# Local attention with two key tiles: the mask added by VectorE together with the maximum

## The reference, cut to what matters

```python
qb = q.reshape(B, H, nb, bs, dk)                 # bs = window = 128
kw = jnp.concatenate([kp[:, :, :-1], kp[:, :, 1:]], axis=3)   # the tile before, the own tile
scores = jnp.einsum('bhnrd,bhncd->bhnrc', qb, kw) * scale
dist = bs + r - c
key_global = i * bs - bs + c
valid = (dist >= 0) & (dist <= window) & (key_global >= 0)
scores = jnp.where(valid[None, None], scores, jnp.finfo(scores.dtype).min)
probs = jax.nn.softmax(scores, axis=-1)
out = jnp.einsum('bhnrc,bhncd->bhnrd', probs, vw)
```

## Time and profile before

| | |
|---|---|
| three runs | 428.84, 430.21, 435.47 us (median 430.21) |
| the profiled execution | 430.3 us, its span 428.5 us |
| mean granted TensorE clock | 0.941 of full speed |
| busy, share of the span | PE 84%, PEld 53%, DVE 72%, ACT 48%, POOL 26% |
| stage 4's 24 items | about 132.8 to 226 us of the span |

### The profile page before, as it was taken

How to read it: one execution, slowest core, us unless ns; L and a number is a source line. 1 busy time by engine, 2 the same in 40 slices (tenths; PEclk the granted TensorE clock), 3 DMA queues, 4 the chain that set the end, 5 groups by cost and what they waited for, 6 DMA issues and landing times.

```text
span 428.5 us, 6958 instructions
## 1 busy us (share of the span) xinstructions
PE 361.4 (84%) x2412; PEld 226.6 (53%) x2438; DVE 307.1 (72%) x652; ACT 207.2 (48%) x549; POOL 110.3 (26%) x214
## 2 busy tenths in 40 slices
PE   8897958699977999989977566678989889999992
PEld 3544646544434576656654332436756645677682
DVE  4998788999725487897888987797988365323245
ACT  2773401260035665775544757889999443110100
POOL 8437777656571000000020111121111000000003
PEclk9999985979999599999998979899999999999998
DMA  7994111731670000020015698999979700511221
GB/s 208 388 366 85 3 1 1 223 72 24 151 315 0 2 2 2 0 50 2 2 27 75 121 162 164 153 165 150 158 142 161 226 3 14 147 49 50 73 74 49
DMA packets 90306, 43.52 MB, mean 102 GB/s; under 512 B 78944, under 2 KB 86048, under 8 KB 89824
## 3 DMA queue, kind: packets, MB, share of 16 engines
q1 hardware_dynamic: 87968, 43.02, 42.8%
q0 software_dynamic: 2304, 0.07, 1.5%
HBM read 21.58 MB, written 2.88 MB: 57 GB/s over the span
## 4 chain that ended last, share of the span: by engine, by line
PE 50%; DVE 14%; DMA 11%; issue 9%; ACT 9%; POOL 5%; SPq 1%; POOLq 0%; DVEq 0%; ACTq 0%
PE ps L833 25%; DMA area_b<-area_a 6%; PE ps L1308 6%; ACT area_a L743 5%; PE ps L1067 5%; PE ps L1078 4%; POOL deltas L536 3%; PE ps L997 2%; PE ps L1061 2%; DMA early<-in_w_qkv_dram 2%; DMA area_b<-deltas 2%; DVE area_a L1700 2%; ACT area_a L718 2%; DMA deltas<-entry_w,small 1%; DVE stats L1431 1%
## 5 line engine op out<-in xcount | busy, mean ns | idle before, releaser
L1700 DVE CUSTOM_DVE_ANT_0 area_a<-ps,zero,small 128x1024 f32<-128x1024 f32 x64 | 79.6, 1275 | 11.2 <-PE ps L1128 8.3
L743 ACT ACTIVATE area_a<-area_a,small 128x1024 int16<-128x1024 f32 x64 | 73.2, 1144 | 21.9 <-POOL small L592 12.8
L718 ACT ACTIVATE area_a<-ps,small 128x256 f32<-128x256 f32 (+1 forms) x128 | 52.0, 430 | 31.9 <-DVE small L1642 28.2
L833 PE MATMUL ps<-xT_odd,early 128*128 128x128 f32 (+2 forms) x248 | 61.8, 393 | 4.7 <-ACT area_a L754 1.9
L514 POOL TENSOR_SCALAR var_eps<-meanvar 128x1 f32<-128x1 f32 x24 | 7.5, 313 | 187.4 <-DVE meanvar L1432 187.3
L833 PEld LDWEIGHTS ps<-xT_odd,early 128*128 128x128 f32 x248 | 38.7, 191 | 26.0 <-ACT area_a L754 5.5
L1642 DVE TENSOR_REDUCE small<-ps 128x4 f32<-128x1024 f32 (+1 forms) x24 | 29.3, 1221 | 20.2 <-PE ps L1067 20.1
L592 POOL TENSOR_SCALAR small<-small 128x1 f32<-128x1 f32 x64 | 12.7, 198 | 87.8 <-DVE small L1700 87.6
L833 PE MATMUL ps<-area_b,xT_even 128*128 128x512 f32 x64 | 30.0, 633 | 5.0 <-ACT area_b L695 5.0
L1783 DVE TENSOR_TENSOR area_b<-ps,area_b 128x384 f32<-128x384 f32 (+1 forms) x16 | 9.2, 573 | 33.7 <-ACT area_b L801 33.7
L1651 DVE COPY area_b<-ps 128x512 f32<-128x512 f32 x48 | 30.9, 680 | 1.6 <-PE ps L1078 1.4
(11 more groups left out here) (285 smaller groups left out, 633.4 us busy)
## 6 DMA issues: line engine op xcount, KB each, us to landing
early<-in_w_up_dram SPq DMA_DIRECT2D x1, 4096.0 KB, 12.6
area_b<-gates_out SPq DMA_DIRECT2D x16, 256.0 KB, 3.0
deltas<-area_b SPq DMA_DIRECT2D x1, 2112.0 KB, 14.6
area_b<-deltas SPq DMA_DIRECT2D x2, 1024.0 KB, 6.3
area_a<-in_w_down_dram SPq DMA_DIRECT2D x1, 2048.0 KB, 9.5
area_b<-area_a SPq DMA_TRANSPOSE x67, 3.3
early<-in_ctxT_dram SPq DMA_DIRECT2D x1, 1024.0 KB, 11.2
early<-in_ctx_dram SPq DMA_DIRECT2D x1, 1024.0 KB
```

Of the source, the lines that this page charges most:

```text
L718: a = act.activation(p1[:, n % 2, x * nk * P:(x + 1) * nk * P], scores1(n)[:, x * nk * P:(x + 1) * nk * P], ACT.Exp, bias=nmx1[:, n % 2, x ...
L743: act.activation(px[:, u % PX, :], sx[:, u % 3, :], ACT.Exp, bias=nbx[:, u:u + 1], accum_out=zx[:, i, h:h + 1]).then_inc(sem("px_ready"), 1)
L833: mm = pe.matmul(dst, lhsT(c), rhs(c), start=start and c == 0, stop=stop and c == DC - 1, **kw)
L1700: dve.tensor_tensor_reduce(sx[:, u % 3, :], bank(2 * (u % 2), 2), zero[:].broadcast_to([P, B * M]), qsc[:, i, h:h + 1], LOWEST, ALU.add, A ...
```

## The change

For items of an odd tile, TensorE no longer writes the mask; the products of queries and keys begin their banks (`start=True`). VectorE, in place of the one maximum, runs one `tensor_tensor_reduce` a head over 256 columns: it adds `window` to the scores, negates the sum, writes it to SBUF into the item's place for weights, and takes the minimum, which is the negated maximum. ScalarE then takes the exponentials in place, SBUF to SBUF, with `scale=-1`. Scores(n+2) wait for `max1_ready` of item n instead of `p1_ready` if item n is of an odd tile. The place for weights is now one of three (`weights1`), the third in `area_b`; who first writes it waits for the turn of item n-3 (`p1_free`). Items of an even tile keep mask, maximum, exponentials and wait as they were, with the three places.

```diff
-        p1 = carve("a", 18 * N, [2, 8 * P])
+        p1 = [carve("a", 18 * N, [8 * P]), carve("a", 20 * N, [8 * P]), carve("b", 10 * N, [8 * P])]
...
+        def masked_by_vector(n):
+
+            return items1[n][0] % 2 == 1
+
+        def weights1(n):
+            return p1[n % 3]
+
+        def p1_free(eng, n):
+
+            if n >= 3:
+                eng.wait_ge(sem("pT1_ps"), 2 * (n - 2))
+
+        def scores1_free(eng, n):
+
+            if masked_by_vector(n):
+                eng.wait_ge(sem("max1_ready"), n + 1)
+            else:
+                eng.wait_ge(sem("p1_ready"), 2 * (n + 1))
...
                     act.wait_ge(sem("max1_ready"), n + 1)
-                    if n >= 2:
-
-                        act.wait_ge(sem("pT1_ps"), 2 * (n - 1))
+                    p1_free(act, n)
+                    by_vector = masked_by_vector(n)
+                    src = weights1(n) if by_vector else scores1(n)
...
-                        a = act.activation(p1[:, n % 2, x * nk * P:(x + 1) * nk * P], scores1(n)[:, x * nk * P:(x + 1) * nk * P],
-                                           ACT.Exp, bias=nmx1[:, n % 2, x:x + 1], accum_out=z1[:, i, h:h + 1])
+                        own = slice(x * nk * P, (x + 1) * nk * P)
+                        a = act.activation(weights1(n)[:, own], src[:, own], ACT.Exp, scale=-1.0 if by_vector else 1.0,
+                                           bias=nmx1[:, n % 2, x:x + 1], accum_out=z1[:, i, h:h + 1])
...
                     if n >= 2:
-
-                        pe.wait_ge(sem("p1_ready"), 2 * (n - 1))
+                        scores1_free(pe, n - 2)
                     heads = slice(hh * HU // nk, (hh + 1) * HU // nk)
-                    for x in range(2):
-                        pe.matmul(bank(2 * (n % 2) + x), ident_b[:], window[:, nk - 1, :], start=True, stop=False)
+                    by_vector = masked_by_vector(n)
+                    if not by_vector:
+                        for x in range(2):
+                            pe.matmul(bank(2 * (n % 2) + x), ident_b[:], window[:, 0, :], start=True, stop=False)
...
-                                           start=False, stop=b == nk - 1)
+                                           start=by_vector, stop=True)
...
+                    if masked_by_vector(n):
+                        p1_free(dve, n)
+                        for x in range(8 // nk):
+                            own = slice(x * nk * P, (x + 1) * nk * P)
+                            m = dve.tensor_tensor_reduce(weights1(n)[:, own], scores1(n)[:, own], window[:, 1, 0:nk * P], -1.0, -LOWEST,
+                                                         ALU.add, ALU.min, nmx1[:, n % 2, x:x + 1])
+                        m.then_inc(sem("max1_ready"), 1)
+                        return
```

More of the change, by code:

```diff
@@ L1077, in turn @@
                         for y in range(4):
-                            mm = pe.transpose(bank(4 + x)[:, y * P:(y + 1) * P], p1[:, n % 2, (4 * x + y) * P:(4 * x + y + 1) * P], ident[:])
+                            mm = pe.transpose(bank(4 + x)[:, y * P:(y + 1) * P], weights1(n)[:, (4 * x + y) * P:(4 * x + y + 1) * P], ident[:])
                         mm.then_inc(sem("pT1_ps"), 1)
```

## The result

| kernel | median us | lowest to highest | ratio to before, 95% interval |
|---|---|---|---|
| before (beside the first series) | 430.36 | 428.84 to 435.47 | |
| changed, first series | 426.71 | 424.15 to 430.56 | 0.9898 [0.9851, 0.9944] |
| changed, repeat (e1_again) | 427.51 | 423.38 to 435.73 | 0.9926 [0.9888, 0.9965] |
| changed, third series (e11_changed) | 427.09 | 422.42 to 429.86 | 0.9896 [0.9820, 0.9971] |

The change makes the kernel faster by 0.7 to 1.0%, 3 to 4.5 us. 425.2 us was forecast, 1.2% less than before. The ratios leave out executions in the chip's slower state, the first profiled one of the changed kernel (430.56 us) among them, while the medians hold all. Lengths of stretches are read from the repeats' profiles where nothing else is said.

The account below looks back on a forecast made before the run. TensorE was taken to bound the odd-tile stretches, the engines coming out level after the change. Gains of 2.9 and 2.5 us, less 0.3, took 430.3 to 425.2 us; own range 423.7 to 426.6, 8-in-10 range 423.0 to 432.0.

Parts of the forecast that it names:

- TensorE full, VectorE with 6 us to spare: Odd-tile stretches of local attention: TensorE busy 26.36 of 27.0 and 26.57 of 27.1 us, VectorE with 6 us left in each.
- 0.43 us of masks an item: Two mask products of 512 columns taken off TensorE per odd item: 3.4 us a stretch, 6.9 us in all.
- 0.35 us a head, from the 512-column row: VectorE's step per 256-column fused operation, ends 0.33 and 0.40; four take 1.41 us for 1.14, +0.27 an item.
- No penalty for exponentials out of SBUF: ScalarE reading the fused result from SBUF: no penalty to be seen, and even 0.1 us more on each hidden.
- The pair at 5.3 us: Two successive odd-tile items in the chain of waits: 5.3 us against 6.15 before.
- The walk: Stepping VectorE and TensorE through a pair of items at the new prices: free at 3.2 us, done at 3.4.
- the lump "for what neither can hide": First odd stretch: 1.2 us added to the fuller engine's 22.9, for waits in four pairs and VectorE's normalising work.
- The piece between only shifts: Even-tile items between the odd stretches keep masks and waits; item 16's scores still wait 2.92 us, this piece only shifts.
- The sum, 5.1 us: Total stage gain: 2.9 us in the first odd stretch, 2.5 in the second, less 0.3 for the last maximum.
- The whole gain is let through: Stage 5, behind the changed stage, is a chain of queues without a fixed date; the whole gain reaches the end.
- rival (a): VectorE's heads cost 0.40 us, +0.46 an item: gain 3.1 us, time 427.1 us; chance 0.19.
- The clock rival (e): TensorE's granted clock falls in a stretch because it waits more; 10 us of work at half speed: 435 us; chance 0.04.

Follow-up runs that it names:

- e11_changed: The changed kernel itself a third time, no edit, timed beside the kernel with both fillings: 427.09 us, ratio 0.9896.
- e2: Kernel before with TensorE's mask products left out for odd tiles and nothing in their place, so those rows are unmasked: ratio 0.9852, 6.4 us.
- e3: Changed kernel with TensorE's mask products put back for the odd tiles, so the mask is added twice: ratio 1.0004.
- e4: Changed kernel with one fused operation of 1024 columns for each odd item in place of four of 256: ratio 0.9916, 426.81 us.
- e11: Short spelling for the third series of the changed kernel, no edit: 427.09 us, ratio 0.9896.
- e10: Changed kernel with the first filling alone, 11 unread TensorE products of 512 columns behind the scores of item 1: ratio 0.9895.
- e7: Kernel before with both fillings, unread TensorE products: 11 of 512 columns behind item 1's scores, 8 of 256 ahead of item 16's: ratio 1.0031.

## Why the prediction was right, point by point

- **TensorE full, VectorE with 6 us to spare**: right for the first stretch, shown by e2 (TensorE's work off: 6.4 us) and e3 (VectorE's on, TensorE's kept: nothing). In the second the 6 us were an average: for 8 us VectorE was full as well (under e2), which the table doesn't show.
- **0.43 us of masks an item**: right on average, 6.42 us for 15 items in e2. It is 0.47 where TensorE alone is late: behind an apply the masks held 0.38 us and the 0.16 of issue ahead of it, 0.54, and 0.43 at the other item. Behind item 16 it is 0.37.
- **0.35 us a head, from the 512-column row**: right to the hundredth. Step 0.345, because the accumulator read does overlap with the next head, as in all rows of before; an item's maximum costs 1.38 us for 1.14. The last hundredths were luck: the 0.35 was taken with one column per nanosecond, which no row shows (the rows' slope is 0.58 us for 512 columns, 1.13 ns each, and gave 0.33). The row of the other fused operation at the right width (0.40) was the wrong one to trust; the same operation at the wrong width was nearer. The Trainium skill's formula for VectorE out of PSUM ("VectorE: DVE Perf Modes", The TRN2 errata) gives an estimate of 0.39 us for 256 columns, between this step and the 0.42 of a single operation's duration; the measured step decides, and it is cheaper. Worked out again, the forecast by that formula would be 1.8 us later, not 1.5.
- **No penalty for exponentials out of SBUF**: there is one. A duration grows by 24 to 28 ns (501 and 497 for 473), and the step from one head's start to the next by 0.04 us, from 0.45 to 0.49 (152.27 and 152.72 before, 167.29 and 167.78 in e1_again). That is 0.16 us an item, hidden as the bound of 0.1 each had allowed: in e1_again the odd items' scores are held up by the exponentials at one place only, the gap ahead of item 16, as before. The Trainium skill ("VectorE: DVE Perf Modes", The TRN2 errata) states a larger fixed part for ScalarE out of SBUF than out of PSUM, 224 against 172 cycles, an estimate of 43 ns at its 1.2 GHz; the step agrees with it, the duration shows a bit over half.
- **The pair at 5.3 us**: 5.18 where TensorE is late; where VectorE is, 159.10 - 153.41 = 5.69 between the maxima of items 5 and 7 in e1_again, of which 0.26 + 0.28 are the tile's own work (the reciprocal and a copy). The walk ended with VectorE waiting 0.2 us on TensorE and left that work to the lump "for what neither can hide".
- **That lump, 1.2 us in the first stretch, is the term that was mis-sized.** Against the masks' 3.4 us a stretch it left a loss of 0.5 us in the first and 0.9 in the second. The runs show 1.07 and 0.68 (the table under e2). In the first stretch it was too small by about 0.6 us; e4, with 0.18 us less on VectorE for each item, got 0.95 of the 1.07 back.
- **The piece between only shifts**: it became 0.84 us shorter. 0.55 of it is item 16's masks, which stood in the chain behind ScalarE's release (0.60 us to the first score product) and which the prediction had counted in the second stretch; the rest, 0.29, is the maximum of item 12, for which VectorE is late in the changed kernel.
- **The sum, 5.1 us**: forecast were 5.4 for 16 items, less 0.3 for the last maximum; measured are 4.68 for 15 of them, less 0.24. Item 4's masks lie in the piece from item 0, whose length varies too much from profile to profile to show them.
- **The whole gain is let through**: right. From item 23's maximum to the end are 211.5 and 211.2 us in the two profiles of before, 211.6 and 211.3 in e1_again and e11.
- **The time**: 426.71, 427.51 and 427.09 us are all a little above the forecast's own range (423.7 to 426.6) and nearer to rival (a)'s 427.1 than to 425.2. That it isn't (a) is known from the step of 0.345 us, not from the time.
- **The clock rival (e), at 0.04**: it came true in single executions, and with it one of the prediction's own signs of being wrong, a clock under 0.95 in a stretch. I argued that the 3 us without TensorE in the chain ahead of 189.77 had cost nothing. Behind the same gap (TensorE idle for 0.92 us before, for 0.91 in the changed kernel) the clock stood at 0.51 for 14 us in the first profile of the changed kernel, which made the second stretch 5.5 us longer, and it fell there in e4's. But a stage gain of 4.4 us (4.68 less 0.24) would be a ratio of 0.990, inside all three intervals, so the times show no loss that the clock has to explain. In none of the three profiles of kernels with all masks and without fillings (two of before, e3) did it fall there; with so few profiles it isn't shown that the change makes the fall likelier.

**What stays open.** That filled gaps are worth some 3 us in the changed kernel is seen in two series (0.9825 and 0.9827 against 0.9898, 0.9926 and 0.9896). In their profiles 2 us lie in the piece from item 0 to item 4 (11.3 us for 13.3), but so they do in e10's. Where the gain comes from, whether it takes both fillings, and why the kernel before gains nothing from them isn't shown: the profiles show what the clock did in one execution, not how often it falls. The fastest version tried is the changed kernel with both fillings, 422.53 us, 0.9827 of before; one fused operation on top (0.9818) can't be told from it.

## What to carry to other kernels

When two engines come out level after a change, price the change by the sum of the fuller one plus what they take from each other, and get that part from a run in which the load is taken off one of them (here 1.1 us in 24). A stretch's average of idle time can hide a piece in which an engine is full, as VectorE was here for 8 us. For the price of an operation at a width that the trace lacks, take the same operation at another width, start to start and not its duration, before another operation at the same width. A time that scatters by more than the gain is worth a look at the granted clock by stretch: lengths between two fixed instructions of the stage repeated to 0.04 us here, while the median of the whole moved by 0.8. And count what lies between the two instructions: a stretch of eight items, measured from its first maximum to the next stretch's, held the scores of only seven of the eight.

## What the runs showed of the hardware that I had not expected

- TensorE's granted clock can drop to its lower level behind a wait of 0.91 us and stay there for 14 us of unbroken work (13.98 of 14.00 us busy at 0.51), in one execution of a program and not in the next (1.00 at the same place in e1_again).
- The same filled gaps, products that nobody reads, went with a ratio of 0.983 for 0.990 to 0.993 in one kernel and made a near twin (e7, 1.0031) no faster, though both show the higher clock where they were put in.
- Four fused operations of 256 columns in a row, each with its accumulator read, run at 0.345 us a step where each lasts 0.419, and the reads of 81 ns add nothing to that step.
